# Attention stage of an audio layer: tiles of the dot products, order of the maxima, form of the denominators

## The reference, cut to what matters

```python
q, k, v = (qkv[0], qkv[1], qkv[2])
qgr, _ = jnp.linalg.qr(q)
kgr, _ = jnp.linalg.qr(k)
attn_grass = jnp.einsum('bhnd,bhmd->bhnm', qgr, kgr) ** 2 * grassman_scale
dots = jnp.einsum('bhnd,bhmd->bhnm', q, k)
attn_eucl = dots * scale
attn_riem = dots ** 2 * riem_scale
a = jnp.concatenate([attn_eucl, attn_riem, attn_grass], axis=1)
a = (a - bn_mean[:, None, None]) * inv + bn_beta[:, None, None]
a = jnp.einsum('oc,bcnm->bonm', conv_w, a) + conv_b[None, :, None, None]
a = jax.nn.softmax(a, axis=-1)
out = jnp.einsum('bhnm,bhmd->bhnd', a, v)
```

## Time and profile before

| quantity | value |
|---|---|
| median of 3 runs | 1039.53 us (1038.96 to 1039.94) |
| the profiled execution, its own time | 1039.8 us |
| its span, first to last instruction | 1038.1 us |
| mean granted TensorE clock | 0.941 of full speed |
| TensorE, VectorE, ScalarE, GpSimd busy | 89%, 73%, 39%, 48% of the span |

### The profile page before, as it was taken

One profiled execution on the slowest core, in us unless ns is written; L12 is line 12 of the kernel. 1 busy time (PEld: TensorE's weight loads), 2 busy tenths in 40 slices (PEclk: granted clock), 3 DMA queues, 4 the chain that ended last, 5 costly groups with the idle time before them and its releaser, 6 DMA issues. The chain is left out here.

```text
span 1038.1 us, 38252 instructions
## 1 busy us (share of the span) xinstructions
PE 919.1 (89%) x15147; PEld 599.2 (58%) x15147; DVE 760.2 (73%) x1336; ACT 400.7 (39%) x647; POOL 500.9 (48%) x567
## 2 busy tenths in 40 slices
PE   4677678998929999999999999999999998889995
PEld 2233245555626666666666666666666665557673
DVE  4588964887965888888888888888888888645552
ACT  2333422113604444444444444444444443224442
POOL 3355631110026666666666666666666663023440
PEclk8788888998968999999999999999999999889997
DMA  8665000325001111111111111111111110000111
GB/s 302 250 224 193 1 0 4 60 53 134 0 19 53 52 51 51 51 51 50 48 48 47 49 48 51 49 51 51 51 51 51 51 47 23 1 0 21 33 33 33
DMA packets 64446, 63.25 MB, mean 61 GB/s; under 512 B 37081, under 2 KB 55068, under 8 KB 64412
## 3 DMA queue, kind: packets, MB, share of 16 engines
q1 hardware_dynamic: 63884, 61.25, 20.1%
q10 hardware_dynamic: 528, 1.54, 0.4%
HBM read 52.93 MB, written 6.75 MB: 57 GB/s over the span
## 5 line engine op out<-in xcount | busy, mean ns | idle before, releaser
L1177 ACT ACTIVATE sq<-ps_dot 128x752 f32<-128x752 f32 x192 | 153.1, 797 | 302.5 <-PE ps_dot L1056 302.5
L1056 PE MATMUL ps_dot<-q_st,k_blk 32*64 32x94 f32 x6144 | 169.5, 247 | 3.0 <-POOL k_blk L1016 3.0
L1056 PEld LDWEIGHTS ps_dot<-q_st,k_blk 32*64 32x64 f32 x6144 | 134.4, 133 | 64.6 <-issue 50.0
L1016 POOL TENSOR_TENSOR k_blk<-k_turn,hmask 128x384 f32<-128x384 f32 x64 | 65.5, 1023 | 177.4 <-ACT k_turn L1165 177.4
L1224 DVE TENSOR_REDUCE sums<-prob 128x94 f32<-128x564 f32 x128 | 147.9, 1199 | 2.0 <-ACT prob L1170 2.0
L1020 POOL TENSOR_TENSOR k_mix<-k_cm,cols 128x768 f32<-128x768 f32 x64 | 119.9, 1873 | 0.0
L1002 POOL TENSOR_TENSOR v_blk<-v_rep,vmask 128x384 f32<-128x384 f32 x128 | 106.6, 854 | 6.8 <-PE ps_m L1088 6.8
L1105 PEld LDWEIGHTS ps_a<-q_st,k_mix 64*64 64x64 f32 x3072 | 77.2, 132 | 56.4 <-issue 48.2
L1105 PE MATMUL ps_a<-q_st,k_mix 64*64 64x94 f32 x3072 | 101.0, 250 | 0.8 <-DVE prob L1212 0.8
L1170 ACT ACTIVATE prob<-prob,cols 128x564 f32<-128x564 f32 x128 | 91.1, 758 | 20.4 <-DVE prob L1212 20.4
L1195 DVE TENSOR_REDUCE row_max<-ps_a 128x94 f32<-128x564 f32 x128 | 89.3, 741 | 12.4 <-PE ps_a L1124 12.4
(11 more groups left out here) (222 smaller groups left out, 1419.3 us busy)
## 6 DMA issues: line engine op xcount, KB each, us to landing
v_rep<-v_rows SPq DMA_DIRECT2D x256, 96.0 KB
x_g<-in_x_dram SPq DMA_DIRECT2D x15, 1500.0 KB, 6.6
v_rows<-tok SPq DMA_DIRECT2D x32, 96.0 KB
q_st<-q_cm SPq DMA_DIRECT2D x64, 47.0 KB, 1.8
out_dram<-rows SPq DMA_DIRECT2D x16, 188.0 KB
x_g<-in_x_dram ACTq DMA_DIRECT2D x1, 1500.0 KB, 7.4
top_rows<-tok SPq DMA_DIRECT2D x16, 32.0 KB
top<-top_rows SPq DMA_DIRECT2D x1, 512.0 KB, 3.5
```

What stands on the lines that cost most here:

```text
L1016: return pool.tensor_tensor(k_blk[:, a, :, kind], view.unsqueeze(2).broadcast_to([128, NTAU, 4, 8]), k["hmask4"][:].unsqueeze(1).unsqueeze ...
L1056: mm = pe.matmul(ps_dot[64 * hg:64 * hg + 64, (a + g) % 2, b, col:col + N], k_blk[rows, a, 2 * (2 * g + t2) + mi].rearrange("p k h m -> p ...
L1177: act.activation(sq[:, :, :, 2 * g:2 * g + 2, :].rearrange("p mi b t n -> p b mi (t n)"), ps_dot[:, (a + g) % 2, :, 0:4 * N].rearrange("p ...
```

## The change

It touches `attend`, and two lines of the constants.

1. **Dots.** Two halves of 24 matmuls instead of three groups of 16. The column half is `64 * (hg ^ mi)`: with the four row groups that makes eight array tiles, and batch and `mi` have a bank of `ps_dot` each. All four banks serve one half, so the second half waits for the squares of the first. For `mi` = 1 the halves of the rows are swapped, and `mix_w` gets a second copy with its rows in that order.
2. **Maxima.** Turn and spread go batch by batch, batch 0 in a free part of `ps_a`'s middle bank, batch 1 in `ps_m`; the turned keys move from `ps_dot` to `ps_m`. The keys are turned right behind the first half of the dots, then come turn 0, a wait for ScalarE's copy of the keys, turn 1, spread 0 and spread 1, then the second half.
3. **Shift.** ScalarE writes it (`shift_out`), one instruction a batch. VectorE subtracts with one instruction a batch over all six `t`. The gap of the padded key moves into the bias of a separate exponential for `t` = 5, so a batch has two exponentials (470 and 94 columns).
4. **Sums.** VectorE adds `t` = 0 to 2 and 3 to 5 into `halves`; TensorE sums the three with `den_w`, 6 matmuls instead of 2.

The core of the diff:

```diff
-            def dots(i, a, g):
...
-                                col = N * (2 * mi + t2)
-                                mm = pe.matmul(ps_dot[64 * hg:64 * hg + 64, (a + g) % 2, b, col:col + N],
-                                               k_blk[rows, a, 2 * (2 * g + t2) + mi].rearrange("p k h m -> p (k h m)"),
+            def dots(i, a, half):
...
+                if half or later(i, 1):
+                    pe.wait_ge(s["squared"], 2 * i + half)
+                for t3 in range(3):
...
+                                at = 64 * (hg ^ mi)
+                                mm = pe.matmul(ps_dot[at:at + 64, b, mi, N * t3:N * t3 + N],
+                                               k_blk[rows, a, 2 * (3 * half + t3) + mi].rearrange("p k h m -> p (k h m)"),
...
+            def turn_max(prev, b):
+                pe.wait_ge(s["max_done"], 2 * prev + 2)
+                pe.transpose(max_bank(b, slice(0, N), 128), top[:, b, :], k["ident"][:]).then_inc(s["max_turned"], 1)
+
+            def spread_max(prev, b):
+                pe.wait_ge(s["max_ready"], 2 * prev + b + 1)
+                pe.matmul(max_bank(b, slice(0, 128), N), top_e[:, b].rearrange("n mi o m -> n (mi o m)"), k["ident"][0:N, 0:N],
+                          start=True, stop=True, is_transpose=True).then_inc(s["max_spread"], 1)
...
+                for t in range(3):
+                    for b in range(2):
+                        mm = pe.matmul(ps_m[64 * b:64 * b + 64, DEN_AT:DEN_AT + N], k["den_w"][:], halves[:, a, b, t, :],
+                                       start=(t == 0), stop=(t == 2))
...
             def step(i, a, has_prev, has_prev2, has_next):
                 dots(i, a, 0)
-                if has_prev:
-                    turn_max(i - 1)
-                dots(i, a, 1)
-                if has_prev:
-                    spread_max(i - 1)
-                dots(i, a, 2)
                 if has_next:
                     turn_keys(i + 1, 1 - a)
+                if has_prev:
+                    turn_max(i - 1, 0)
+                    if has_next:
+                        pe.wait_ge(s["kt_out"], i + 2)
+                    turn_max(i - 1, 1)
+                    for b in range(2):
+                        spread_max(i - 1, b)
+                dots(i, a, 1)
...
+            def shift_out(prev, b):
...
+                act.activation(shift[:, b, :], max_bank(b, slice(0, 128), N), ACT.Identity, bias=k["conv_const"]).then_inc(s["max_out"], 1)
+
+            def exps(prev, a, b):
+                act.wait_ge(s["sub_done"], 2 * prev + b + 1)
+                act.activation(prob[:, a, b, 0:5], prob[:, a, b, 0:5], ACT.Exp, bias=k["conv_const"])
+                act.activation(prob[:, a, b, 5], prob[:, a, b, 5], ACT.Exp, bias=k["pad_bias"][:]).then_inc(s["exp_done"], 1)
...
+                    dve.wait_ge(s["max_heads"], 2 * prev + b + 1)
+                    dve.tensor_copy(top_e[:, b], top_o[:, b].unsqueeze(1).unsqueeze(3).broadcast_to([N, 2, H, 8])).then_inc(s["max_ready"], 1)
...
+            def sums_of(prev, a, b):
+                dve.wait_ge(s["exp_done"], 2 * prev + b + 1)
+                dve.tensor_tensor(halves[:, a, b], prob[:, a, b, 0:3], prob[:, a, b, 3:6], ALU.add).then_inc(s["sum_done"], 1)
```

More of the change, by code:

```diff
@@ L957, in attend @@
         prob = sb("prob", [128, 2, 2, NT, N])
-        sums = sb("sums", [128, 2, N])
+        halves = sb("halves", [128, 2, 2, 3, N])
         inv = sb("inv", [128, N])
@@ L1037, in turn_keys @@
                 pe.wait_ge(s["m_ready"], i + 1)
[L1038 to L1041, removed]
-            def dots(i, a, g):
-                if g == 0:
+                if later(i, 4):
+                    pe.wait_ge(s["out_done"], i - 3)
+                pe.matmul(ps_m[:, KT_AT:KT_AT + NP], m_blk[:, a].rearrange("p q d -> p (q d)"), k_cm[:, span(i, 1), :],
+                          start=True, stop=True, skip_group_check=True).then_inc(s["kt_done"], 1)
+            def dots(i, a, half):
+                if half == 0:
                     pe.wait_ge(q_in[a], 16 * ((i - a) // 2 + 1) if isinstance(i, int) else 8 * (i - a) + 16)
@@ L1075, in attended @@
                 pe.wait_ge(s["v_ready"], j + 1)
-                pe.wait_ge(s["shift_done"], j + (1 if last else 2))
+                pe.wait_ge(s["max_out"], 2 * j + (2 if last else 4))
                 pe.wait_ge(s["out_done"], j)
@@ L1151, in _ @@
             steps(pe, step)
-            turn_max(PAIRS - 1)
-            spread_max(PAIRS - 1)
+            for b in range(2):
+                turn_max(PAIRS - 1, b)
+            for b in range(2):
+                spread_max(PAIRS - 1, b)
             attended(PAIRS - 2, 0, False)
-            denominators(PAIRS - 2, None)
+            denominators(PAIRS - 2, 0, None)
             attended(PAIRS - 1, 1, True)
-            denominators(PAIRS - 1, None)
+            denominators(PAIRS - 1, 1, None)
         @block.scalar
@@ L1181, in step @@
                 if has_prev:
-                    exps(i - 1, 1 - a)
+                    act.wait_ge(s["mixed"], 2 * i)
+                for b in range(2):
+                    squares(i, 0, b)
+                if has_prev:
+                    for b in range(2):
+                        shift_out(i - 1, b)
+                    exps(i - 1, 1 - a, 0)
+                for b in range(2):
+                    squares(i, 1, b)
+                if has_prev:
+                    exps(i - 1, 1 - a, 1)
             turned_out(0, 0)
             steps(act, step)
-            exps(PAIRS - 1, 1)
+            for b in range(2):
+                shift_out(PAIRS - 1, b)
+            for b in range(2):
+                exps(PAIRS - 1, 1, b)
         @block.vector
@@ L1212, in shifted @@
-                dve.scalar_tensor_tensor(out=prob[:, a, :, 5, :], in0=bass.AP(ps_a[:].tensor, A_AT + 5 * N, [[3 * 512, 128], [B_AT - A_AT, 2], [1, N]]),
-                                         scalar=k["pad_col"][:], in1=shift[:], op0=ALU.subtract, op1=ALU.subtract).then_inc(s["sub_done"], 1)
+                for b in range(2):
+                    dve.wait_ge(s["max_out"], 2 * prev + (b + 1))
+                    dve.tensor_tensor(prob[:, a, b], all_logits(b, [[N, NT], [1, N]]), shift[:, b, :].unsqueeze(1).broadcast_to([128, NT, N]),
+                                      ALU.subtract).then_inc(s["sub_done"], 1)
```

138 lines of the change are left out of this document (57 added, 81 removed).

## The result

| | median | ratio to before, 95% interval |
|---|---|---|
| before | 1039.66 us (1038.96 to 1039.94, 4 runs) | |
| changed | 1113.7 us (1111.71 to 1115.92, 4 runs) | 1.071 (1.069 to 1.074) |

The changed kernel is 74 us slower. The forecast was 1056.5 us with a range to 1067: the direction was right, the size not. Of the loss, 17 us were foreseen; 57 were not. The profiled execution took 1113.69 us, its span is 1112.0.

The account below looks back on a forecast made before the run. TensorE was taken to bound the kernel. Terms gave -0.23 us a step, but with GpSimd holding the second copy the step became 9.15 against 8.88 us: 62 x 0.27 = +17 us, so 1056.5 us, range 1018 to 1067.

Parts of the forecast that it names:

- the granted clock still 1.00: Sign expected in the changed profile: TensorE's clock stays at its upper level, 2.4 GHz.
- Dots: TensorE's 96 dots passes in two halves on eight tiles, rounds of 0.08 us, starts over 0.50 each: -0.91 us a step.
- The held copy: In the exchange of maxima, GpSimd's k_blk holds VectorE's second widening copy from 2.19 to 2.70, 0.51 us; chance 0.50.
- T: Start of a step's first dots on TensorE, from which the prediction counts times in the exchange of maxima.
- The step: Step length closed over GpSimd and TensorE with the second copy held: 9.15 us against 8.88, +0.27.
- Heads: VectorE's maxima over heads, 0.42 us for 256 columns, become two of about 0.29 us.
- shift: The shift goes to ScalarE, at 0.33 us each, 0.66 us a step.
- additions: VectorE's two sum reductions of 1.20 us become additions of 0.45 us each: -1.5 us of VectorE work.
- Twelve denominator passes: TensorE's denominators go from 4 passes to 12 on two tiles, 4 more rounds: +0.32 us a step.
- Not held: Rival: GpSimd does not hold the widening copies; -0.23 us a step, 1025 us; chance 0.29.
- Door kept: Rival: k_blk follows k_mix so closely that the first copy waits for both; step 9.7 us, 1091 us; chance 0.11.
- Tiles: Rival: eight tiles don't run together, each dots half 0.98 us; 1064 to 1120 us; chance 0.07.

Follow-up runs that it names:

- e9: The changed kernel, copy still held, with three useless matmuls between the two spreads of the maxima, where TensorE stands waiting; 1064.3 us.
- e1: The changed kernel with VectorE widening the maxima by a reduction over an axis of one element instead of a copy, so it is not held; 1045.7 us.
- e3: e1 with the earlier kernel's VectorE reductions for the sums and two denominator matmuls instead of six; 1028.3 us.
- e2: The changed kernel with the dots back on four array tiles instead of eight; 1121.3 us.
- e5: e1 with two more maxima over heads ahead of batch 1's in every step, lengthening the exchange of maxima; 1125.8 us.
- e6: e1 with the dots on four array tiles instead of eight; 1080.7 us.
- e10: e8 with e1's reduction for the widening and e3's old sums; 1036.2 us.
- e7: The changed kernel, copy still held, with eight useless matmuls between the two spreads of the maxima; 1124.2 us.
- e8: The changed kernel with the turn of the keys moved from the exchange into the mixing, and GpSimd building v_blk before the turned keys' k_blk; 1121.8 us.
- e11: e8 with e1's reduction for the widening, keeping the changed kernel's new sums; 1052.6 us.

## Why the prediction was wrong

By its own steps:

- **The failed step: "the granted clock still 1.00".** The sum took each duration at the clock of the earlier trace rows, with no term and no rival for the clock itself, while it lengthened the waits and shortened the dots between them. Measured is 0.89 in 400 to 800 us, steps of 10.23 us in the mean, and e9 prices this at 49.4 us, most of the 57.2 missed. e1 and e3 show that the dots alone don't do it, e2 that a longer stop on four tiles does it in one step of 38, e5 that both together do it again and again, without GpSimd. What in TensorE's work decides is open.
- **Dots, mis-sized.** -0.91 us a step from rounds of 0.08 on eight tiles. A half starts over 0.63 us, not 0.50, so the term is -(1.91 - 1.26) = -0.65. "A round takes 0.08 us whether two or four tiles work in it" is true of two and four (e6: 12 rounds in 0.96) and was drawn on too far. The rule of the Trainium skill that I weighed (TensorE: Matmul & The Clock Gate, "The mechanism", Part 3), as I read it, would have no gain at all; e6 against e1 measures 35 us of gain. The truth lies between my term and that reading.
- **The held copy, right.** `k_blk` of the turned keys at T + 1.81 to 2.82 (forecast 1.82 to 2.84); the first copy free, 0.22; the second ends at T + 2.91 (2.70 + 0.22 = 2.92). The wait of TensorE is 0.81 (0.9). The second copy was ready 0.17 later than forecast (T + 2.36, not 2.19), so it lost 0.33 us and not 0.51; its end didn't move, as `k_blk` sets it. The contention that the Trainium skill names (SBUF — State Buffer, "Who interferes with whom") is borne out in 62 of the 64 pairs, not once.
- **The step, nearly right at its clock.** e9, the changed kernel at full clock with its stop filled, has 9.29 us; forecast 9.15. The difference is the dots: from the second half to the attention product 0.88 us (501.92 to 502.80 in e9) where the sum had 0.50 + 0.17. Denominators to scores 0.61 (0.44 + 0.17) fits. So does 1064.3 against 1056.5.
- **Small terms.** Heads 0.29 (0.287), shift 0.33 (0.34), ScalarE 5.4 us a step (four squares of 0.631, two exponentials of 0.685 and two of 0.361, two shifts of 0.34, 0.25: 5.5), additions 0.45 alone. Twelve denominator passes +0.32 (e3: 0.28, e10: 0.26). All stood. A slip in the range: its lower end of 1046 us is a step of 8.99 by the sum's own rule, not 9.04; nothing hangs on it.
- **The rivals.** *Not held* was put at 1025; the kernel that fulfils its condition, e1, takes 1045.7, 8.99 us a step for 8.65. From T to the second half it has 2.93 us (500.89 to 503.82) where the forecast had 2.66, and from there to the attention product 0.81 where it had 0.67: the slower dots twice, and two widenings of 0.28 instead of 0.22. *Door kept* is refuted, but not by the steady step, where no copy waits with another instruction behind the one that holds it. It happens early in the changed kernel (and once in e2, e7 and e9): `v_blk` stands right behind `k_blk`, and the waiting copy still ends 0.08 behind `k_blk`:

```profile
320.45 1.02 POOL L1034 TENSOR_TENSOR k_blk<-k_turn,hmask 128x384 f32<-128x384 f32 x1
...
320.93 0.62 DVE L1226 COPY row_max_e<-row_max_o 94x128 f32<-94x128 f32 x1
321.44 1.65 POOL L1017 TENSOR_TENSOR v_blk<-v_rep,vmask 128x384 f32<-128x384 f32 x2
```

  A held *first* copy, which that rival was about, arises all the same where the exchange comes late against GpSimd (e2, e8). *Tiles* ran from 1064 (four-tile speed, nothing held) to 1120 (held): the first is e6, 1080.7, the second e2, 1121.3, while the changed kernel, on eight tiles, reached 1114 by another road, and that it lies near 1120 is chance.

## What to carry to other kernels

A full clock in the profile of before is an input of the forecast, not a constant: where an edit makes matmul groups shorter and the waits between them longer, keep a rival with the clock at its lower level, and price it (here 49 us of 1040). Look for the stretches of before where the clock did fall, as here at 324 us, and for what stood ahead of them. An engine off the critical path can hold another (here GpSimd a copy of VectorE, 0.55 us for 0.22); an operation in a form that isn't held (here a reduction over one element, 0.28 us for 0.22) is a cheaper cure than a new order. Take the parts of a change one by one: here new order and tiles, with the old sums and a widening that isn't held, were 1% faster than before, and the whole was 7% slower.

## What the runs showed of the hardware

- **The clock falls without a long stop.** No stop of TensorE in the changed kernel's step is longer than 0.81 us, and it falls to 1.2 GHz all the same. The Trainium skill tells of a kernel whose clock swings because TensorE idles briefly again and again (TensorE: Matmul & The Clock Gate, "A second HAM failure mode: psum-queue depth-cycling"); this trace agrees, 1.00 and 0.50 in turn. Of the kernels with eight tiles and no fill e1, e3, e10 and e11 keep the clock, and the changed one, e5 and e8 lose it. Length of step isn't what parts them: every second step of e11 takes 9.3 us, longer than the shortest of the changed kernel (9.22), and e2 has 10.2 with four tiles. Nor is it the length of one stop alone: TensorE waits up to 0.84 us in e10 (at 508.15) and keeps the clock. What quantity decides is left open.
- **Eight tiles:** 48 passes start over 0.63 us, 13 ns each, against 20 on four tiles (e6). What limits them wasn't tried.
- **A slowdown that is no lock.** The later addition of a step, beside GpSimd's `v_blk` and `m_blk`, takes about twice its 0.45 us, and `m_blk` 0.62 instead of the 0.41 that it takes in e8 (the timelines of the changed kernel and of e8). The addition ends 0.32 us behind `v_blk` (507.55 to 509.21), less than the 0.45 it needs alone, so part of it ran beside `v_blk`. The Trainium skill counts instructions of VectorE with two SBUF inputs among what meets GpSimd (GPSIMD Engine Reference, "1. Specifications"); here the addition and `m_blk` are slowed. Ahead of e1 I had said that additions lose nothing beside GpSimd; this one does. A cost to the step doesn't show: e1 and e3 differ by no more than the rounds of the denominators.

```profile
508.57 0.96 DVE L1245 TENSOR_TENSOR halves<-prob 128x282 f32<-128x282 f32 x1
...
509.17 0.62 POOL L1024 TENSOR_TENSOR m_blk<-m_t,mask 128x128 f32<-128x128 f32 x1
```

```profile
511.99 0.41 POOL L1024 TENSOR_TENSOR m_blk<-m_t,mask 128x128 f32<-128x128 f32 x1
```
